# Attention's q and k through DRAM in another layout, six transfers back in place of twelve, and the v product in the middle of a turn

## What is computed

```python
x = x + 0.5 * ffn(layernorm(x))
qkv = layernorm(x) @ (s1 * W_qkv)
q, k, v = split(qkv)                         # 16 heads of 8 features
att = softmax(where(causal, q @ k.T / sqrt(8), -big))
x = x + (att @ v) @ (s2 * W_proj)
x = x + 0.5 * ffn(layernorm(x))
```

## Time and profile before

| what | value |
|---|---|
| time before, median of 3 | 1400.01 us (1397.74 to 1402.59) |
| profiled execution | 1410.97 us, of which 1409.2 us is the span that the trace shows |
| busy share of the span | PE 74%, DVE 52%, ACT 43%, POOL 46% |
| attention | about 464 to 1034 us of the span |

### The profile page before, as it was taken

How to read it: one execution, slowest core, us unless ns; L and a number is a source line. 1 busy time by engine, 2 the same in 40 slices (tenths; PEclk the granted TensorE clock), 3 DMA queues, 4 the chain that set the end, 5 groups by cost and what they waited for, 6 DMA issues and landing times. The chain is left out here.

```text
span 1409.2 us, 29547 instructions
## 1 busy us (share of the span) xinstructions
PE 1038.8 (74%) x8359; PEld 792.5 (56%) x8390; DVE 732.6 (52%) x2124; ACT 601.4 (43%) x1498; POOL 648.9 (46%) x1022
## 2 busy tenths in 40 slices
PE   2496636877775568888888888888875835778676
PEld 1385416767765245555555555555544615777676
DVE  5476782222221457667777767777535792222222
ACT  4023303433443145556666666666552403434334
POOL 3250005666654135555555555555440005666664
PEclk9657857988988589999999999999996956999898
DMA  4250001111110233333333333333200001111110
GB/s 135 84 160 0 0 2 42 41 39 41 42 38 27 75 84 89 92 88 96 91 91 91 95 98 91 92 96 95 72 17 4 0 0 39 40 44 41 38 41 23
DMA packets 115112, 83.72 MB, mean 59 GB/s; under 512 B 13307, under 2 KB 105523, under 8 KB 115030
## 3 DMA queue, kind: packets, MB, share of 16 engines
q1 hardware_dynamic: 95638, 59.44, 15.4%
q0 software_dynamic: 9216, 18.15, 5.1%
q10 hardware_dynamic: 10176, 5.11, 1.2%
HBM read 52.23 MB, written 30.67 MB: 59 GB/s over the span
## 5 line engine op out<-in xcount | busy, mean ns | idle before, releaser
L1288 DVE TENSOR_REDUCE at_mx<-at_pp 128x2 f32<-128x512 f32 (+1 forms) x384 | 259.9, 685 | 144.8 <-remote 78.7
L1039 POOL TENSOR_SCALAR_AFFINE_SELECT at_pt<-at_pt 128x256 f32<-128x256 f32 (+1 forms) x384 | 187.5, 495 | 239.9 <-ACT at_pt L1081 236.8
L1081 ACT ACTIVATE at_pt<-at_pm 128x512 f32<-128x512 f32 x384 | 226.4, 598 | 134.7 <-PE at_pm L1153 76.2
L807 ACT ACTIVATE e_ht<-e_ps_h,b1t 128x128 f32<-128x128 f32 x576 | 164.2, 378 | 226.9 <-remote 97.2
L775 POOL DMA_INDIRECT e_x<-rows,gidx x144 | 140.1, 973 | 242.0 <-issue 143.3
L835 PE MATMUL e_ps_h<-e_xnt,e_w1own 128*128 128x128 f32 x1152 | 178.2, 304 | 67.7 <-issue 42.3
L845 PE MATMUL e_ps_y<-w,e_ht 128*128 x1152 | 187.6, 303 | 31.6 <-issue 31.3
L835 PEld LDWEIGHTS e_ps_h<-e_xnt,e_w1own 128*128 128x128 f32 x1152 | 162.9, 218 | 75.4 <-issue 50.4
L881 DVE SCALAR_TENSOR_TENSOR e_y<-e_ps_y,e_x 128x256 f32<-128x256 f32 x72 | 30.6, 425 | 312.1 <-PE e_ps_y L845 192.5
L845 PEld LDWEIGHTS e_ps_y<-w,e_ht 128*128 128x128 f32 x1152 | 160.6, 210 | 40.8 <-issue 38.1
L1174 PE MATMUL at_po<-at_pt,vp 128*32 128x256 f32 (+1 forms) x2048 | 111.1, 335 | 1.0 <-POOL at_pt L1039 1.0
(11 more groups left out here) (257 smaller groups left out, 1748.7 us busy)
## 6 DMA issues: line engine op xcount, KB each, us to landing
at_qkd<-at_part SPq DMA_DIRECT2D x64, 192.0 KB, 2.9
kb<-at_qkd SPq DMA_DIRECT2D x64, 96.0 KB
qs<-at_qkd SPq DMA_DIRECT2D x64, 96.0 KB
rows<-ts_x ACTq DMA_DIRECT2D x16, 264.0 KB, 3.4
rows<-at_x SPq DMA_DIRECT2D x32, 132.0 KB, 2.4
ts_x<-in_x_dram SPq DMA_DIRECT2D x16, 256.0 KB, 3.3
at_xa<-x SPq DMA_DIRECT2D x32, 128.0 KB, 2.8
kb<-at_qkd SPq DMA_DIRECT2D x64, 64.0 KB
```

Source lines behind the costliest of these rows:

```text
L807: last = a.activation(hid_t[j % NB][:, f, :], ps_h[j % NB][:, f, :], ACT.Gelu, bias=c.b1t[:, ds(e, 1), f])
L1039: g.affine_select(out=tile, in_=tile, compare_op=ALU.is_ge, fill=0.0, base=0, pattern=[[0, n], [1, P]], channel_multiplier=-1).then_inc(ma ...
L1081: a.activation(pt[u % RING][:, :], pm[u % 2], ACT.Exp, scale=SCALE).then_inc(exped, 1)
L1288: v.tensor_reduce(out, src, axis=AX.X, op=ALU.max).then_inc(maxed, 1)
```

## The change

q goes to one DRAM buffer and k to another (`qd`, `kd`). `kd` has for each row two runs of 256 tokens, one for each head of a pair, and the run of the wrong head holds zeros, stored once in the preamble. So k comes back with its zeros in whole rows of 8 KB, and q in rows of 4 KB. There are three transfers out and six back. The rows of both heads now alternate in groups of 8, and q and k still meet in the same 96 rows. The bytes read back are 393 KB for q as before and 786 KB for k in place of 393.

The splitting of q and k and the product for v come one unit earlier, and the work on sequence b-2 comes later and has its transposes in `mi[0]` behind the v product. In the preamble VectorE's memsets of `kb` go. One activation is left of four, and `kb[0]` is copied to the other three by transfers on ScalarE's queue, which also store the zeros in `kd`.

```diff
@@ preamble
+            g.memset(c.kb[0][0:48, :, :, :].bitcast(F32), 0.0).then_inc(cleared, 1)
...
-            for k in range(NQ):
-                nc.scalar.activation(c.kb[k][ROWS:P, :, :, :], sel[ROWS:P, :].unsqueeze(1).unsqueeze(3).to_broadcast([P - ROWS, HP, 2, S]),
-                                     ACT.Copy).then_inc(minus, 1)
+            nc.scalar.activation(c.kb[0][ROWS:P, :, :, :], sel[ROWS:P, :].unsqueeze(1).unsqueeze(3).to_broadcast([P - ROWS, HP, 2, S]),
+                                 ACT.Copy).then_inc(minus, 1)
+            act.wait_ge(minus, 1)
+            for k in range(1, NQ):
+                act.dma_start(c.kb[k][ROWS:P, :, :, :], c.kb[0][ROWS:P, :, :, :]).then_inc(laid, 16)
+            act.wait_ge(cleared, 1)
+            for h in range(2):
+                act.dma_start(io["kd"][h].rearrange("(a g) z n -> a g z n", g=HP), c.kb[0][0:48, :, :, :]).then_inc(laid, 16)
...
+            act.wait_ge(laid, 16 * (NQ - 1 + 2))
...
-                v.memset(c.kb[k][0:ROWS, :, :, :].bitcast(F32), 0.0).then_inc(minus, 1)
@@ attention, SyncE
-                    for r in range(2):
-                        sp.dma_start(qkd[h][6 * 64 * r:6 * 64 * (r + 1), :].rearrange("(t w) n -> w t n", t=6),
-                                     part[h][64 * r:64 * r + 64, :, :]).then_inc(part_out[h], 16)
-                    wait(sp, part_out[h], dma_count(n, 2, 2)(h))
-                    src = qkd[h].rearrange("(a g) n -> a g n", g=HP)
-                    for r in range(2):
-                        for row, size in ((0, 24), (24, 16), (40, 8)):
-                            to, q0, k0 = 48 * r + row, 48 * r, 48 * (r + 1) - size
-                            sp.dma_start(kb[q][to:to + size, :, r, :], src[k0:k0 + size, :, :]).then_inc(qk_in[q], 16)
-                            sp.dma_start(qs[q][to:to + size, :, :], src[q0:q0 + size, :, :]).then_inc(qk_in[q], 16)
+                    sp.dma_start(qd[h].rearrange("(t w) n -> w t n", t=3), part[h][:, 0:3, :]).then_inc(part_out[h], 16)
+                    k_to = kd[h].rearrange("(t r w) z n -> r z w t n", t=3, r=2)
+                    for r in range(2):
+                        sp.dma_start(k_to[r, r, :, :, :], part[h][64 * r:64 * r + 64, 3:6, :]).then_inc(part_out[h], 16)
+                    wait(sp, part_out[h], dma_count(n, 2, 3)(h))
+                    q_from = qd[h].rearrange("(a g) n -> a g n", g=HP)
+                    k_from = kd[h].rearrange("(a g) z n -> a g z n", g=HP)
+                    for to, size in ((0, 48), (48, 32), (80, 16)):
+                        sp.dma_start(qs[q][to:to + size, :, :], q_from[0:size, :, :]).then_inc(qk_in[q], 16)
+                        sp.dma_start(kb[q][to:to + size, :, :, :], k_from[48 - size:48, :, :, :]).then_inc(qk_in[q], 16)
@@ attention, where the small work stands (unit before -> unit after)
   PE   L1193/L1194 q and k product 2 -> 1;  L1206 v product 4 -> 3
   ACT  L1092 first terms 2 -> 1;  L1105 second terms 4 -> 3;  L1109 copy of v 5 -> 4
   DVE  L1300 rest 3 -> 2;  POOL L1050 third terms 5 -> 4
   DVE  L1272 xn2 2 -> 4;  PE L1190 transposes 3 -> 5;  ACT L1087 3 -> 5;  PE L1200 and ACT L1095 6 -> 7
@@ attention, PE, unit 5, ahead of L1215
+                    if u == 5 and has(-2):
                         wait(pe, xn2_done, (b - 1) * TPB)
+                        if has(3):
+                            wait(pe, v_out, b + 4)
+                        else:
+                            wait(pe, mt_out, b + 1, B)
                         for j in range(TPB):
-                            te.transpose(mi[1][:, j * P:(j + 1) * P], xn2[k % 2][:, j, :], c.ident[:, :]).then_inc(x2t_tr, 1)
+                            te.transpose(mi[0][:, j * P:(j + 1) * P], xn2[k % 2][:, j, :], c.ident[:, :]).then_inc(x2t_tr, 1)
```

More of the change, by code:

```diff
@@ L250, in _ @@
             for k in range(NQ):
[L251 to L252 removed]
+                v.memset(c.qs[k][ROWS:P, :, :].bitcast(F32), 0.0).then_inc(blank, 1)
             v.memset(gelu_b1[:, :], 0.0).then_inc(filled, 1)
@@ L935, in attention @@
         mi = [t.ps(f"at_mi{k}", [P, 2 * S]) for k in range(2)]
-        qkd = [nc.dram_tensor(f"at_qkd{k}", (6 * P, S), BF16, kind="Internal").ap() for k in range(2)]
+        qd, kd = io["qd"], io["kd"]
         xa_in, xr_in, row_out = ([sem(f"{n}{k}") for k in range(2)] for n in ("xa_in", "xr_in", "row_out"))
@@ L1046, in turn @@
                         g.tensor_tensor(c.xnorm[:, ds(n * TPB, TPB)], x2[q][:, :, D + 1], x2[q][:, :, D + 2], ALU.mult).then_inc(xnorm_done, 1)
-                    if u == 5 and has(3):
+                    if u == 4 and has(3):
                         q = (k + 1) % 2
@@ L1084, in turn @@
                         a.activation(xt[(k + 1) % 2][:, :], mi[0][:, 0:S], ACT.Copy).then_inc(xt_out, 1)
-                    if u == 3 and has(-2):
+                    if u == 5 and has(-2):
                         wait(act, x2t_tr, (b - 1) * TPB)
-                        a.activation(x2t[k % 2][:, :], mi[1][:, 0:S], ACT.Copy).then_inc(x2t_out, 1)
-                    if u == 2 and has(3):
+                        a.activation(x2t[k % 2][:, :], mi[0][:, 0:S], ACT.Copy).then_inc(x2t_out, 1)
+                    if u == 1 and has(3):
                         h = (k + 1) % 2
                         wait(act, qk_mm, b + 4)
-                        wait(act, part_out[h], dma_count(b + 1, 2, 2)(h))
+                        wait(act, part_out[h], dma_count(b + 1, 2, 3)(h))
                         a.activation(part[h][:, 0:6:5, :], mi[0].rearrange("p (a n) -> p a n", a=2), ACT.Copy).then_inc(a_done, 1)
-                    if u == 6 and has(-2):
+                    if u == 7 and has(-2):
                         wait(act, num_mm, b - 1)
@@ L1101, in turn @@
                                      ACT.Copy).then_inc(ot_out, 1)
-                    if u == 4 and has(3):
+                    if u == 3 and has(3):
                         h = (k + 1) % 2
@@ L1130, in scores_by_query @@
                     if v == 0:
-                        wait(pe, qk_in[s], dma_count(n, NQ, 12)(s))
+                        wait(pe, qk_in[s], dma_count(n, NQ, 6)(s))
                     wait(pe, maxed, n * NP + (v - 1))
@@ L1194, in small @@
                         te.matmul(mi[0][:, S:2 * S], c.wk[:, :], xt[(k + 1) % 2][:, :], start=True, stop=True).then_inc(qk_mm, 1)
-                    if u == 6 and has(-2):
-                        wait(pe, x2t_out, b - 1)
-                        wait(pe, v_out, b + 4, B)
-                        pe.sem_inc(passed, 1)
-                        for j in range(TPB):
-                            last = te.matmul(mi[0][:, j * E:(j + 1) * E], x2t[k % 2][:, j * P:(j + 1) * P], c.waff_t[:, :],
-                                             start=True, stop=True)
-                        last.then_inc(num_mm, 1)
-                    if u == 4 and has(3):
+                    if u == 3 and has(3):
                         wait(pe, r_done, b + 4)
@@ L1210, in small @@
                         wait(pe, ot_out, b)
-                        wait(pe, x2t_out, b - 1)
+                        wait(pe, x2_done, b - 1)
                         for j in range(TPB):
@@ L1221, in small @@
                         last.then_inc(ont_tr, 1)
+                    if u == 7 and has(-2):
+                        wait(pe, x2t_out, b - 1)
+                        for j in range(TPB):
+                            last = te.matmul(mi[0][:, j * E:(j + 1) * E], x2t[k % 2][:, j * P:(j + 1) * P], c.waff_t[:, :],
+                                             start=True, stop=True)
+                        last.then_inc(num_mm, 1)
                     if u == 8 and has(-1):
@@ L1291, in turn @@
                         statistics(b - 2, x2[q], bn2[q], vare2[q], bnd2, mv2, var2, True)
-                    if u == 2 and has(-2):
+                    if u == 4 and has(-2):
                         wait(dve, rstd2, b - 1)
@@ L1295, in turn @@
                         normalise(xn2[k % 2], x2[k % 2], xn2_done)
-                    if u == 3 and has(3):
+                    if u == 2 and has(3):
                         h = (k + 1) % 2
@@ L1341, in macaron @@
         io["rows"] = nc.dram_tensor("rows", (T, XW), F32, kind="Internal").ap()
+        io["qd"] = [nc.dram_tensor(f"at_qd{k}", (3 * P, S), BF16, kind="Internal").ap() for k in range(2)]
+        io["kd"] = [nc.dram_tensor(f"at_kd{k}", (3 * P, 2, S), BF16, kind="Internal").ap() for k in range(2)]
         x1 = nc.dram_tensor("x1", (T, D), F32, kind="Internal").ap()
```

7 lines of the change are left out of this document (4 added, 3 removed).

## The result

| | before | after |
|---|---|---|
| median (lowest to highest) | 1401.3 us (1397.7 to 1404.5) | 1533.4 us (1527.5 to 1541.0) |
| ratio, 95% interval | 1 | 1.095 [1.088, 1.101] |
| profiled execution: span, mean clock | 1409.2 us, 0.865 | 1525.8 us, 0.834 |

The change makes the kernel 9.5% slower. The forecast was 2.7% faster.

The account below looks back on a forecast made before the run. The ring of q and k transfers was taken to bound each 17.06 us turn. Gains of 30 us (turns), 3.3 (first read) and 5 (preamble), 38 in all, took 1400.0 to 1362 us; range 1345 to 1386.

Parts of the forecast that it names:

- the ring of q and k: Attention: third term, stores, reads, first query tile and back to the next third term; 13.67 + 3.39 us sets the 17.06 us period.
- The wait on q and k: First query tile's wait for transfers, 45.8 us over 29 turns; goes because the ring would run over two turns, period (D + 17)/2.
- D: Time from the third term's end to the first query tile: 13.67 us before, 10.4 forecast; bounds the turn from 15.2 on.
- Reads at 0.66 us an issue: SyncE's queue in attention: six reads at the old issue cost, whatever their bytes, 3.94 us in all.
- landing 1.99: Attention: from the last read's issue to the first query tile, 1.99 us, taken unchanged from the trace before.
- First read: Sequence 0, where nothing hides the transfers: 13.67 - 10.4 = 3.3 us gained.
- waits that come: New TensorE waits in a turn: about 1.0 us in unit 5, 0.1 us in unit 1, none in unit 3.
- The turn itself: Steady attention turn: from 17.1 to 16.1 us, bounds 15.5 and 17.0; 30 us over 30 periods.
- The wait in unit 5: TensorE's transposes of xn2 wait for ScalarE's copy of v: 0.9 us a turn, 1.0 with the semaphore.
- The other waits: TensorE's waits on the rest (L1300) and on xn2 before the transposes go: 0.5 us a turn.
- Preamble: VectorE's chain starts 5.9 us earlier without memsets; expert weights in at 26 to 27.5; gain 5 us, between 3 and 5.9.
- The one on the slower side: Rival: reads go by their bytes in attention, D 19.2, period 18.1 us, time 1431 us; chance 0.05.

Follow-up runs that it names:

- e2: Kernel before with only the small work moved to the changed kernel's units; preamble, layout, two stores and twelve reads kept: 1381.7 us, ratio 0.982.
- e3: Changed kernel (new layout and preamble) with the small work back in the units of the kernel before: 1384.1 us, ratio 0.984.
- e1: Changed kernel with the six reads held until the same turn's transfer of the row maxima has landed: 1444.3 us, ratio 1.026 to the kernel before.
- e10: Changed kernel with reads dealt to every second row and held until the exponential of unit 9 is done: 1253.0 us, ratio 0.960 to the kernel before.
- e8: New layout and preamble, small work in the old units, reads dealt to every second row: 1254.9 us, ratio 0.960 to the kernel before.
- e7: Changed kernel with the same reads dealt to every second row: 1344.4 us, ratio 1.026 to the kernel before.
- e9: Changed kernel itself, unaltered, run again on the other chip: 1441.3 us, ratio 1.104 to the kernel before.
- e11: Changed kernel with its three pairs of reads in reverse order, 16 rows first and 48 last: 1342.9 us, ratio 1.031 to the kernel before.

## Why the prediction was wrong

- *What bounds the kernel before.* Right: the ring of q and k set the turn. The new places open it (e2), the layout alone shortens it (e3, where the first tile still waits for k), and either is worth 1.6 to 1.8% alone.
- *"The wait on q and k goes even if the reads get no faster."* Right: one such wait is left. D measured 12.8 us (707.89 to 713.68 + 7.0 = 720.7), over the forecast of 10.4 and under the bound of 15.2.
- *Reads at 0.66 us an issue.* They take 0.34 to 0.60, 2.84 us for six, where 3.94 stood. The error is in the term behind it: "landing 1.99". The last read lands 7.0 us after the start of its issue, since the engines move data at 178 GB/s there (1180 KB would take 6.6 us). The 299 GB/s set against it came from the preamble's loads, whose rows aren't these. Reads with landing are 3.3 us over, the stores and what lies before them 0.9 under; together it is 2.4 us of D, which the two-turn ring absorbs.
- *First read.* 0.7 us in place of 3.3: from the first third term to the first tile are 12.9 us (458.63 to 471.52), where 13.6 stood (465.31 to 478.92).
- *The step that failed.* The part on waits that come went through ScalarE's unit 4, unit 5 and unit 1, and not through the other transfer that TensorE waits for each turn. The third term moved one unit ahead pulled the reads ahead of the maxima's issue in unit 8; two stores and twelve reads had also been a brake, and with six reads that went too. That put up to 704 KB in front of 24 KB which had 2.6 us to arrive (712.73 to 715.37) and need 2.4 on empty engines. The price is 4.6 us of waiting and 2.1 put down to the halved clock in each of 25 turns, 168 us in all over turns of 16.1, where the forecast took 30 off. The slack could have been read in the trace of before:

```profile
708.19 0.74 ACTq L1120 DMA_DIRECT2D qs<-at_mt  x1
```

There the maxima are issued 0.85 us ahead of the first read (709.04) and 2.9 us behind the third term (705.24). In the changed kernel they come 4.8 us behind it (707.89 to 712.73): a shift of 1.9 us, more than the lead.
- *The turn itself.* Right as far as two turns show: 15.98 and 16.64 us where the maxima weren't behind the reads, against 16.1. *The wait in unit 5*: 0.9 us against 0.9. *The other waits* (L1300, L1272) went.
- *Preamble.* VectorE's chain was right to 0.2 us. The weights came at 31.1, not at 26 to 27.5: the 1.58 MB were taken to fill an idle stretch, but their transfers land 12 us after their issue, in the midst of the weights' own. 1.2 us in place of 5 at the products, 1.5 at the block's end.
- *The rivals.* The one on the slower side had the reads going by their bytes; their slow landing did count, but through another wait than it named. In e1, with the reads moved back, that rival's period is about what came, 18.1 us against 18.3, but by luck in part: its D was 19.2 from bytes alone, that of e1 is 20.4 from reads that start 7.6 us later and land slowly.

What stays open: why e10 is as fast as e8 though it holds the reads back, what exactly decides whether the maxima get ahead when both are issued within some 0.1 us, and whether the preamble's copies, issued behind the weights, would give the other 4 us. None of these was tried.

## What to carry to other kernels

When a change lets one queue issue the same bytes in fewer instructions, list every other transfer whose landing an engine waits for, with the time between its issue and its use, and see what will be issued ahead of it; the bytes ahead divided by the rate in the windows is an estimate of its delay (here good to about 1 us). A slow issuing queue is a brake that spaces the traffic out, and taking it off moves the small, urgent transfer to the back. And where the order of rows is free, deal them over all partitions: against the same kernels without it that was 2.4% (e8 by e3) and 7% (e7 by e9).

## What the runs showed of the hardware

- Transfers into 48, 32 and 16 neighbouring rows keep all 16 engines busy at 178 GB/s (changed kernel, 712 to 721); into every second row the same transfers run at 256 GB/s (e7, 640 to 646). A busy share near 1 is no proof of a full rate.
- A 24 KB transfer on ScalarE's queue lands in 2.4 us alone (e1), and 6.9 to 7.8 us after its issue in the changed kernel's turns with 704 KB from SyncE's queue ahead of it (4.6 us, mostly, behind 320 KB in e11).
- A read of 4 or 8 KB a row takes 0.34 to 0.6 us to issue, about as much as one of 512 B runs a quarter of its size in rows 3 (0.46 to 0.84 us). To every second row it is 0.54 to 0.67 us (e7).
- Behind TensorE's wait of 4.2 us the granted clock was 0.50 for about six us. Behind waits of 1.9 us (e11) and 2.5 us (e7) the key tile's two matmuls took 0.39 us, as at full clock; behind one of 2.1 us early in the changed kernel's trace 0.60, as at half. The wait's length alone doesn't settle it.
